# Attention skewed by a unit with the bias on GpSimd, first normalisation in the front part, residual added by TensorE

## The reference, cut to what matters

```python
q = layernorm(x) @ Wq + bq ;  k, v = split(ctx @ Wkv + bkv)      # per head: [2048, 32]
q = fq_sym(q * 32**-0.5, axis=-1); k = fq_sym(k, axis=-1); v = fq_sym(v, axis=tokens)
p = fq_unsigned(softmax(q @ k.T), axis=-1)       # 255 steps up to the row's largest probability
x = x + (p @ v) @ Wp + bp
h = layernorm(x)
s = sqrt(softplus(h @ router.T)); idx = top4(s + expert_bias); w = s[idx] / sum(s[idx])
x = x + sum_e w_e * expert_e(h) + shared(h)      # expert: (silu(clip(h@g)) * clip(h@u)) @ d
```

## Time and profile before

| | us |
|---|---|
| median of 3 runs (1593.75 to 1603.7) | 1594.2 |
| profiled execution | 1586.03 |
| its span, first to last instruction | 1584.3 |
| busy: PE / DVE / ACT / POOL | 1313.4 / 1043.8 / 852.0 / 822.9 |

### The profile page before, as it was taken

One profiled execution on the slowest core, in us unless ns is written; L12 is line 12 of the kernel. 1 busy time (PEld: TensorE's weight loads), 2 busy tenths in 40 slices (PEclk: granted clock), 3 DMA queues, 4 the chain that ended last, 5 costly groups with the idle time before them and its releaser, 6 DMA issues.

```text
span 1584.3 us, 27888 instructions
## 1 busy us (share of the span) xinstructions
PE 1313.4 (83%) x7826; PEld 663.6 (42%) x7923; DVE 1043.8 (66%) x1943; ACT 852.0 (54%) x1183; POOL 822.9 (52%) x611
## 2 busy tenths in 40 slices
PE   7997777787778778778777748879999998989997
PEld 3443333344444444434443434434444444444443
DVE  6546799999999999999999926733333332323333
ACT  2223699888899889989888932112221121212221
POOL 1001577678877777877776720434443443434441
PEclk9999689888998999888999969999999999999999
DMA  8433467675666566566656546455777666665545
GB/s 228 83 76 60 74 120 127 108 126 113 132 132 121 117 124 126 120 131 131 122 117 112 119 141 231 141 212 117 192 190 230 148 166 189 152 190 126 91 65 158
DMA packets 383108, 216.26 MB, mean 137 GB/s; under 512 B 346007, under 2 KB 346135, under 8 KB 378786
## 3 DMA queue, kind: packets, MB, share of 16 engines
q1 hardware_dynamic: 365186, 177.36, 46.2%
q0 software_dynamic: 17872, 38.29, 13.5%
HBM read 103.42 MB, written 36.70 MB: 88 GB/s over the span
## 4 chain that ended last, share of the span: by engine, by line
PE 28%; DVE 26%; issue 22%; DMA 17%; ACT 3%; DVEq 1%; POOL 1%; POOLq 0%; SPq 0%; ACTq 0%
DVE mem L542 15%; DMA acc_dram<-mem 15%; PE psS L752 11%; PE psS L760 4%; DVE mem L572 3%; PE psS L436 3%; PE psS L1570 2%; PE psAV L407 2%; PE psT L1181 1%; PE psP L1551 1%; ACT mem L495 1%; PE psP L744 1%; DMA mem<-xn_dram,mem 1%; DMA mem<-xn_dram 1%; DVE mem L518 1%
## 5 line engine op out<-in xcount | busy, mean ns | idle before, releaser
L627 POOL TENSOR_SCALAR mem<-mem 128x2048 bf16<-128x2048 uint8 x256 | 485.4, 1901 | 179.2 <-DMA mem<-mem 147.8
L495 ACT ACTIVATE mem<-mem 128x2048 uint8<-128x2048 f32 x256 | 536.1, 2094 | 12.4
L436 PE MATMUL psS<-mem 128*128 128x512 bf16 x929 | 323.1, 425 | 177.7 <-DVE mem L572 126.4
L752 PE MATMUL psS<-mem 128*128 (+1 forms) x752 | 358.7, 620 | 0.1
L572 DVE TENSOR_SCALAR_CACHE_REDUCE mem<-psS,mem 128x1024 f32<-128x1024 f32 x256 | 328.1, 1282 | 23.9
L542 DVE TENSOR_SCALAR_CACHE_REDUCE mem<-psS 128x1024 f32<-128x1024 f32 x256 | 311.8, 1218 | 16.1 <-PE psS L436 15.8
L786 DVE TENSOR_SCALAR mem<-psS 128x512 f32<-128x512 f32 x94 | 65.2, 693 | 344.6 <-PE psS L752 344.6
L1151 POOL DMA_INDIRECT acc_dram<-mem x78 | 124.6, 1597 | 232.5 <-DMA acc_dram<-mem 195.1
L780 ACT ACTIVATE mem<-mem 128x256 f32<-128x256 f32 x94 | 39.3, 418 | 360.2 <-DVE mem L786 360.2
L436 PEld LDWEIGHTS psS<-mem 128*128 128x128 bf16 x1024 | 74.4, 103 | 313.5 <-DVE mem L542 147.5
L752 PEld LDWEIGHTS psS<-mem 128*128 128x128 f32 x752 | 140.5, 197 | 152.5 <-issue 149.8
(11 more groups left out here) (206 smaller groups left out, 1202.9 us busy)
## 6 DMA issues: line engine op xcount, KB each, us to landing
mem<-in_moe_w SPq DMA_DIRECT2D x33, 1536.0 KB, 8.2
mem<-in_x SPq DMA_DIRECT2D x32, 256.0 KB, 3.0
acc_dram<-mem SPq DMA_DIRECT2D x29, 256.0 KB, 2.3
mem<-mem SPq DMA_TRANSPOSE x288, 3.1
xn_dram<-mem SPq DMA_DIRECT2D x17, 256.0 KB, 2.1
mem<-in_ctx_in SPq DMA_DIRECT2D x16, 256.0 KB, 3.2
mem<-xn_dram SPq DMA_DIRECT2D x16, 256.0 KB, 5.0
mem<-acc_dram SPq DMA_DIRECT2D x16, 256.0 KB, 4.2
```

The source lines that it names most:

```text
L436: last = nc.tensor.matmul(psS[c][:, k * D:(k + 1) * D], qT[p][:, h, :], kT[:, h, c * HALF + k * D:c * HALF + (k + 1) * D], start=True, sto ...
L495: nc.scalar.activation(p8[slot], S[slot], ACT.Exp, bias=NB[:, slot:slot + 1], scale=sq[p][:, h:h + 1], accum_out=Z[p][:, h:h + 1]).then_in ...
L627: nc.gpsimd.tensor_scalar(pb[slot], pT[slot].bitcast(U8).rearrange("p (j q b) -> p j b q", b=2, q=P), 1.0, 0.0, ALU.mult, ALU.add).then_in ...
L752: last = nc.tensor.matmul(bankG[o], xT[o if xo is None else xo][:, c, :], w(c * 2 * I, 2 * I), start=(c == 0), stop=(c == DC - 1))
```

## The change

1. **Skew.** In each unit's step PE now makes the first half of unit n and the second half of unit n-1, and DVE evicts them in that order. LAG goes from 6 to 7, BEHIND from 2 to 3.
2. **Bias on GpSimd.** `NB` is computed by POOL, at the head of each step, instead of ACT.
3. **First normalisation in the front part.** DVE's statistics of tile i of `x` now stand ahead of the rounding of key tile i; POOL normalises into the same buffer; SP fetches the tile of `x` and stores the normalised one to `xn_dram`, both behind the transposing DMA of key tile i. In attention SP only fetches from `xn_dram`.
4. **Residual by TensorE.** A product of the identity and `x` is added into the output's bank, and ACT copies the sum out; DVE's addition goes.
5. **Other places for query steps**, and a shorter DVE chain for the scale of the queries: two small DVE operations go, POOL makes two. Three copies of the queries are spread instead of four.

```diff
-    LAG = 6
-    BEHIND = 2
-    OUT_AT = (9, 11, 13, 14)
+    LAG = 7
+    BEHIND = 3
+    OUT_AT = (9, 10, 11, 13, 14)
...
             if stage == 0:
-                pe.wait_ge(xn_ready, t + 1)
+                pe.wait_ge(xn_in, 16 * (t + 1))
...
+            elif stage == 1:
+                pe.wait_ge(x_again, 16 * (t + 1))
+                nc.tensor.matmul(bank[:], ident[:], xr, start=True, stop=False)
+                nc.tensor.matmul(bank[:], ones3[:], bias3[:, 2 * D:3 * D], start=False, stop=False)
...
-            if there(t):
-                scores(1)
+            if within(n - 1):
+                scores(1, n - 1, p if h else 1 - p, (h - 1) % H)
...
+            if h == 13 and there(t - 1):
...
+                nc.scalar.activation(x1, psAV[1 - p][:], ACT.Copy).then_inc(x1_ready, 1)
             if there(t):
                 slot, use = l % NS, (PAIR // NS) * tt + l // NS
-                if h == 0:
-                    act.wait_ge(minus_ready, t + 1)
-                act.wait_ge(half_max[1], n + 1)
-                nc.scalar.activation(NB[:, slot:slot + 1], M[:, 2 * slot + 1:2 * slot + 2], ACT.Identity,
-                                         bias=ln255[:], scale=nsq[p][:, h:h + 1]).then_inc(bias_ready, 1)
                 act.wait_ge(bias_ready, n + 1)
...
             nc.vector.tensor_reduce(amax, hv(psP[:]), AX.X, ALU.max, apply_absolute_value=True).then_inc(q_amax, 1)
-            dve.wait_ge(q_amax, t + 1)
-            nc.vector.tensor_scalar(sq[p], amax, QSCALE / 127.0, 1e-8, ALU.mult, ALU.max).then_inc(q_scale, 1)
...
-            nc.vector.tensor_scalar(rz2, rc, QSCALE, None, ALU.mult).then_inc(q_factor, 1)
...
-                nc.vector.tensor_tensor(x1, psAV[1 - p][:], xr, ALU.add).then_inc(x1_ready, 1)
-            if h == 13:
-                dve_stats(dve, t + 2)
...
-            if there(t):
-                dve.wait_ge(scores_made[1], n + 1)
-                dve.wait_ge(half_max[0], n + 1)
...
+            if within(n - 1):
+                dve.wait_ge(scores_made[1], n)
+                dve.wait_ge(half_max[0], n)
+                nc.vector.tensor_scalar(S[before][:, HALF:TK], psS[1][:], 1.0, M[:, 2 * before:2 * before + 1],
...
-            if h == 8:
-                dve_whole(dve, t + 1)
-            if h == 15 and there(t - 1):
+            if h == 10:
+                dve_whole(dve, t + 1, 1 - p)
+            if h == 0 and there(t - 2):
...
         def pool_step(pool, tt, l):
             n, p, h = PAIR * tt + l, l // H, l % H
             t = 2 * tt + p
+            if there(t):
...
+                pool.wait_ge(half_max[1], n + 1)
...
+                nc.gpsimd.tensor_scalar(NB[:, slot:slot + 1], M[:, 2 * slot + 1:2 * slot + 2],
+                                            nsq[p][:, h:h + 1], LN255, ALU.mult, ALU.add).then_inc(bias_ready, 1)
...
+            if h == 7 and there(t + 1):
+                pool_scale(pool, t + 1, 1 - p)
...
-            if h == 14 and there(t + 2):
-                pool_root(pool, 0, t + 2)
-            if h == 15 and there(t + 2):
-                pool_normal(pool, t + 2)
...
+                    sp.wait_ge(xn_ready, i + 1)
+                    apart(sp, i + 1)
+                    if due(16 * i):
+                        sp.wait_ge(xn_stored, 16 * i)
+                        apart(sp, i)
+                    if prefetch or r < 3:
+                        sp.dma_start(x_buf[(r + 1) % 2], rows(x, i + 1)).then_inc(x_in, 16)
+                    sp.dma_start(rows(xn_dram, i), x_buf[r % 2]).then_inc(xn_stored, 16)
...
                     ps = bankK[r]
+                    dve_stats(dve, i, r % 2)
+                    dve_mean(dve, 0, i)
                     dve.wait_ge(k_mm, i + 1)
```

More of the change, by code:

```diff
@@ L351, in there, with within @@
             return not isinstance(t, int) or 0 <= t < TT
+        def within(n):
+            return not isinstance(n, int) or 0 <= n < TT * H
         block = es.enter_context(nc.Block())
@@ L471, in act_step @@
             t = 2 * tt + p
-            if h == 10 and there(t - 2):
+            if h == 11 and there(t - 2):
                 if due(t - 1):
@@ L536, in dve_step @@
             t = 2 * tt + p
-            slot = l % NS
+            slot, before = l % NS, (l - 1) % NS
             if there(t):
@@ L543, in dve_step @@
                                             accum_out=M[:, 2 * slot:2 * slot + 1]).then_inc(half_max[0], 1)
-            if h == LAG + 1 and there(t - 1):
+            if h == LAG and there(t - 1):
                 if due(H * t):
@@ L617, in pool_step @@
             t = 2 * tt + p
+            if there(t):
+                slot = l % NS
+                if h == 0:
+                    pool.wait_ge(minus_ready, t + 1)
+                    apart(pool, t + 1)
+                pool.wait_ge(half_max[1], n + 1)
+                apart(pool, n + 1)
+                if due(n - NS + 1):
+                    pool.wait_ge(exp_done, n - NS + 1)
+                    apart(pool, n - NS + 1)
+                nc.gpsimd.tensor_scalar(NB[:, slot:slot + 1], M[:, 2 * slot + 1:2 * slot + 2],
+                                            nsq[p][:, h:h + 1], LN255, ALU.mult, ALU.add).then_inc(bias_ready, 1)
             if not isinstance(n, int) or 0 <= n - BEHIND < TT * H:
@@ L658, in sp_step @@
             t = 2 * tt + p
-            if h == 2 and there(t + 2):
-                sp.wait_ge(xn_ready, t + 2)
+            if h == 3 and there(t + 2):
+                sp.wait_ge(query_tr, t + 2)
                 apart(sp, t + 2)
-                sp.dma_start(xt, rows(x, t + 2)).then_inc(x_in, 16)
+                sp.dma_start(xn, rows(xn_dram, t + 2)).then_inc(xn_in, 16)
             if h == 2 and there(t - 1):
                 if due(t - 1):
-                    sp.wait_ge(x1_ready, t - 1)
+                    sp.wait_ge(attn_mm, t - 1)
                     apart(sp, t - 1)
@@ L672, in sp_step @@
                 sp.dma_start(rows(xn2_dram, t - 2)[:, 0:D], xn2).then_inc(xn2_stored, 16)
+            if h == 10 and there(t + 1):
+                sp.wait_ge(q_spread, t + 2)
+                apart(sp, t + 2)
+                if due(H * t):
+                    sp.wait_ge(scores_made[1], H * t)
+                    apart(sp, H * t)
+                sp.dma_start_transpose(qT[1 - p], qst.rearrange("p h j d -> p (h j d)")).then_inc(queries_moved[1 - p], 16)
             if there(t):
@@ L1320, in _ @@
             sp.dma_start(bvT, bv).then_inc(w_kv, 16)
[L1321 removed]
+            sp.dma_start(x_buf[0], rows(x, 0)).then_inc(x_in, 16)
             sp.dma_start(wq_sb, wq.rearrange("(c p) n -> p c n", p=P)).then_inc(w_q, 16)
@@ L1331, in _ @@
             sp.dma_start(ebias_sb[:], ebias.to_broadcast([P, E])).then_inc(r_bias, 16)
+            sp.wait_ge(spare_zero, 16)
             def keys(g, prefetch):
@@ L1349, in _ @@
             keys(GK - 1, False)
-            sp.wait_ge(spare_zero, 16)
-            sp.wait_ge(xn_ready, 1)
-            sp.dma_start(xt, rows(x, 1)).then_inc(x_in, 16)
+            sp.wait_ge(xn_stored, 16 * TT)
+            sp.wait_ge(query_tr, 1)
+            sp.dma_start(xn, rows(xn_dram, 1)).then_inc(xn_in, 16)
             sp.wait_ge(q_spread, 1)
@@ L1384, in _, with normal @@
             pool_constants(pool)
-            pool_root(pool, 0, 0)
-            pool_normal(pool, 0)
+            def normal(t, b):
+                pool_root(pool, 0, t)
+                pool_normal(pool, t, b)
+            for r in range(4):
+                normal(r, r % 2)
+            with pool.Fori(1, GK) as g:
+                for r in range(4):
+                    normal(4 * g + r, r % 2)
             for m in range(DC // 2):
```

127 lines of the change are left out of this document (55 added, 72 removed).

## The result

| | before | changed |
|---|---|---|
| median, 4 runs each (us) | 1593.97 (1587.03 to 1603.7) | 1613.64 (1611.31 to 1622.31) |
| profiled execution, span | 1586.0, 1584.3 | 1612.3, 1610.2 |

The ratio is 1.0161, 95% interval 1.0118 to 1.0204: slower by 1.6%. Four marks on DVE cut the span into parts: the first eviction of a score half, the last second half, the last copy of `logits`.

What follows compares the result with a forecast made beforehand. DVE was taken to set the pace in attention, and a DVE and ACT chain in the front part. +74 + 12 - 53 = +33 on 1586.0 gives 1619; the median, 8 us above, gives 1627 (range 1588 to 1675).

Steps and rivals of the forecast that it cites:

- likeliest case: Whole kernel: slower, net +16 to +60 us, 1610 to 1654 us, chance 0.45.
- Waits for x: Front part: DVE waits for x behind the transposing DMA, then makes statistics; 6.15 us in 12 of 16 key tiles, +74.
- Clock: Front part: PE idles some 18 us longer per group and then runs at half clock; 4 x 3 us, +12.
- Port lock: Front part: DVE's SBUF operations held up by GpSimd's new work; some 10 us possible by the skill, 0 in the sum.
- Attention: Attention: a query tile falls from 46.4 to 42.9 us, less 3 at the pipeline's end; -53 us.
- my own bound of 20: Both parts: prediction wrong if their lengths differ from +86 (front) and -53 (attention) by more than 20 us.
- DVE's floor: Attention: least DVE time per query tile, 16 units of 2.36 us plus 3.2 for other operations, 41.0 us.
- late steps of PE: Attention: PE steps with the residual or the output and router products exceed DVE's unit; about 0.9 us a tile.
- the gap: Attention: DVE's 0.21 us wait per unit for the maximum just made, removed by the skew; unit 2.57 to 2.36.
- Moves costed at 0: Attention: moved DMAs have three or more units to spare, cost 0; without that cover each costs 3 us a tile.
- raise the tile to 46: Attention, rival: GpSimd sets the pace, a tile takes 46 us and attention gains 3; +83, 1677 us, chance 0.25.
- Faster: Whole kernel, rival: attention's gain of 83 us outweighs the front part's lower bound of 63; -20, 1574 us, chance 0.10.

Runs made afterwards that it cites:

- early fetch: The changed kernel with SP's fetch of the next x tile put ahead of its wait for the key tile and the transposing DMA; 1553.4 us, ratio 0.980.
- front undone: The changed kernel with the first normalisation (fetch, statistics, normalising of x) back in attention, the rest kept; 1550.2 us, ratio 0.977.
- skew undone: The changed kernel with both score halves of a unit in the same step again on PE and DVE, the rest kept; 1650.7 us, ratio 1.038.

## Why the prediction was right, and where its sizes were off

The likeliest case came: slower, by two opposite terms, with the front part as the larger. That the sum is as close as it is (+33 forecast, +26 between the profiled executions) is in part luck: the front part was put 8 us too low and attention's gain 20 too low, and the two errors pull opposite ways.

- **Waits for x, +74 forecast.** The mechanism is what happened: 12 waits of 5.4 to 7.3 us (with a shorter one ahead of the first tile 73.8 in 13), released by the fetch of x; the early fetch takes most of them away. The size: the 12 distances between first maxima within a group grew by 84.7 together, 7.06 each against 6.15. In the key tile shown above, 0.4 of SP between its two DMAs, 0.4 of landing (3.39 for 3.0) and 0.2 of statistics and aggregate (84.08 to 85.20 is 1.12, for 0.95) came on top, and 0.1 of issue went. The hand-over between statistics and aggregate is 0.34 there, where the row taken for it has 0.03: it appears in the loop's tiles, not in the first group's, which are written out.
- **Clock, +12 forecast.** What is left of +94.1, 9.4 us, is 1.1 at the start and 1.7 to 2.6 in each of the four stretches of value pieces. The third and fourth pieces together take 8.7 to 9.8 us instead of 7.1, which is all of it but the start. PE idles 23.3 us ahead of the third piece (timeline of PE) and starts it at half clock (stretches):

```profile
115.64 6.91 PE L1589 MATMUL psS<-mem 128*128 128x512 f32 x11 [23.28 <-ACT mem L1452]
```

```profile
115.00:119.00 4.00, 3.37 (x4) 1.51 (x5) 1.97 (x3) 1.16 (x3) 0.00 (x0) 0.50 0.52 100
```

  The long wait is not the only thing that brings the half clock there: with the front undone PE idles 1.9 us at that place, as before, and two of its four groups still take 8.8 us.

- **Port lock, put at 0.** By the page SBUF — State Buffer of the Trainium skill (section "SBUF: two separate sides") some 10 us were possible, an estimate from the durations of L518. The trace agrees that two such operations hold each other up, at a far smaller price for DVE. L1497 has two SBUF inputs and meets GpSimd's normalisation L595. In the first group, where L595 starts 0.45 us ahead, L1497 takes 0.85 us instead of 0.69 (four times, 0.6 us in all). In nine tiles of the loop the two start within 0.1 us of each other or L595 later; there L1497 keeps its 0.69, and L595 takes 0.99 to 1.28 us, where it takes 0.76 in the tiles in which L1497 is not beside it; nobody waits for it. L1499 and L1501 meet no GpSimd work. First group, then loop (timelines of POOL and DVE):

```profile
42.19 0.76 POOL L595 TENSOR_SCALAR mem<-mem 128x512 f32<-128x512 f32 x1
42.64 0.85 DVE L1497 TENSOR_TENSOR mem<-mem 128x512 f32<-128x512 int8 x1
```

```profile
99.76 1.28 POOL L595 TENSOR_SCALAR mem<-mem 128x512 f32<-128x512 f32 x1 [0.21 <-POOL mem L590]
99.79 0.69 DVE L1497 TENSOR_TENSOR mem<-mem 128x512 f32<-128x512 int8 x1
```

- **Attention, -53 forecast, -73.4 measured.** This term failed by my own bound of 20. The bare unit (2.35 for 2.36) and DVE's floor were right: 41.0 forecast; from 400 to 850 us 16 units take 42.1, of which 0.95 is idle time before L547, leaving 41.1. The mis-sized terms are those put over the floor, 0.9 for late steps of PE and 1.0 for a spell at half clock, which made 42.9 a tile. All of DVE's idle time was 0.95: four spells at half clock are left in 10.7 tiles, where the kernel before had about two a tile, and the whole of attention gives 41.8. Why the spells went is open: the kernel with the skew undone has about one a tile (mean clock 0.95) though PE waits at most 1.1 us at once there, as in the changed kernel. The pipeline's end cost 0.2, not 3.
- **The gain of the skew.** The floor prices every unit without the gap and every added operation at its full 0.61, as the earlier trace rows has it, and so comes out right. The skew's own share of it is 2.4 us a tile, since 11 units of 16 had the whole 0.21 and one a half of it; the kernel with the skew undone loses 2.2.
- **Moves costed at 0.** With the kernel as it is they cost nothing that a run shows. But "three or more units to spare" was wrong for the queries: without their move the skew costs 3.9 us a tile, more than the 3 I named, and the whole change would be 5.2% slower. The move is a condition of the skew.
- **Rivals.** GpSimd did not raise the tile to 46, but it is nearly level with DVE: 0.43 a bias, where I had 0.35. Faster needed a front part at its lower bound and a tile under 41.3; the tile came within 0.5, the front part did not.

## What to carry to other kernels

A fetch behind a DMA that waits for the reader's own last operation puts the whole transfer on that reader's path; fetch it one tile further ahead, or issue it before the wait, and look next for the store that frees the buffer. Here that made the difference between 90 us and 1.3 for the same work in the front part. Put small operations where the busy queue already waits for its partner. A skew delays every queue behind the skewed one: list what PE takes from them at fixed places, and move those steps in the same edit.

## What the runs showed that I had not expected

- SP's issue of the transposing DMA of a key tile takes 1.83 us at the median, and 2.88 with a fetch of 256 KB issued just ahead of it; the fetch lands in 2.8 us ahead of that DMA and in 3.6 behind it.
- A two-input DVE operation and a GpSimd operation on SBUF that meet lengthen one another: 0.16 us on DVE where GpSimd was first, up to 0.52 on GpSimd where the two started together.
- A dependent DVE pair (L521, L517) has 0.33 to 0.36 us between its two in the loop, 0.03 to 0.04 in the written-out first group.
- The expert part, untouched, lasted between 642.1 and 656.6 us from one profiled execution to the next, while the front part of equal front code repeats within 3 us and attention within 2 (668.5 to 670.5 in five kernels with the same attention code). Small edits are better told by the part's length than by the median.
